# A fused attention and quantised linear layer: eight more score units among the projections, and a lead of 18 units in place of 14

## The chip, the cores and the metric

The kernel runs on one core of one Trainium2 chip. A core has engines with one instruction stream each, which meet through semaphores: PE (TensorE, matrix products into PSUM), DVE (VectorE), ACT (ScalarE), POOL (GpSimd) and SP (which here issues most DMAs). The metric is the device time of one execution in microseconds (us). The kernel before takes 1662.35 us, the median of three runs from 1661.26 to 1664.51 us. The profiled execution is another run of it.

## The reference, cut to what matters

The input `x` has 2 batches of 2048 tokens with 256 channels; there are 16 heads of 16 channels.

```python
q_in = linear(x, Wq);  Q = linear(concat[q_in, conv1d(q_in, 3 taps)], qproj)     # K in the same way
V = linear(x, Wv)
tau   = sigmoid(conv1d(gelu(depthwise_conv(x)), 1 tap))        # one number per token and head
delta = sigmoid(conv1d(gelu(depthwise_conv(x)), 1 tap))
scores = Q @ K.T / 4 * tau[query] + delta[key]
attn = softmax(scores) @ V
x = layernorm(x + linear(attn, out))
x = layernorm(x + fake_quant(x) @ fake_quant(weight).T + bias)
```

The softmax needs the maximum of each row of `scores`. The kernel computes every score twice: once with queries on the partitions, only to find the row maxima, and once with keys on the partitions, for the exponentials, with the maxima already subtracted inside the matrix product.

## The kernel before, in words

**Two blocks.** The first block (lines 355 to about 730) computes Q, K, V, tau and delta in 8 chunks of 512 tokens, here called chunk 0 to 7. All engines meet at its end. The second block is the loop: 32 iterations `i`, one for each group of four heads and 512 queries, four iterations to a group.

**A score unit** is a pair of matmuls (`s_unit`, the matmuls have line L227) that writes 128 queries by 512 keys for two heads at once into two PSUM banks, and one DVE `tensor_reduce` (`max_unit`, L237) that takes the maxima. An iteration's queries need 32 units, called (j, u) with u from 0 to 31 for iteration j. There are two pairs of banks, so unit s waits on PE until DVE has done the maximum of unit s-2 (semaphore `s_free`). The 1024 units and a few other pieces of work form one list, `items`, which PE and DVE go through in the same order.

**From maxima to rows.** For each j, POOL does 8 folds (`fold`, L248 and L251, four small instructions each), then `split_max` (L85 and L89 on `nm_pad`). DVE then transposes the result (`rows_turn`, L268) and SP stores it as extra rows beside the queries (`rows_store`, L279). DVE waits in `rows_turn(j-1)` for the semaphore `nm_ready`, and this call stands in DVE's program right behind the maximum of unit (j, 1), wherever that unit stands. POOL's folds for j = 0 stand in its program at the head of chunk 7, behind the last `q_sp` work of chunk 6 (L89 on `q_sp`); those for j = 1 stand at the start of the loop, behind a run of small bias copies (L1310 to L1320).

**Where units are done.** Some units are done early, in the first block. `PRE_STEP` says how many at each of 15 places of a chunk: places 0 to 2 and 3 to 5 are behind each six matmuls of the two K projections (L681), 6 behind the first half of the values (L695), 10 behind the second half, 7 to 9 and 11 to 13 in the two Q projections, 14 behind the pointwise product for the next chunk (L704). `DVE_PLACES` sets the points of DVE's order at which the maxima of these places stand, between its convolution taps (L525) and evacuations (`k_lows` L531, `v_bias` L539, `q_scale` L549). `PRE` is the sum, 42 units before.

**The loop's PE order.** An iteration has 32 slots. A slot has half the probabilities-times-values matmuls (`pv_half`, L918), two score matmuls for the exponentials (`st`, L905), and then as many items as `due` asks for: the items up to unit `LEAD` of iteration i+2, evenly over the slots. So iteration 0 does what is missing up to (2, LEAD), 36 units before; others do 32, and iteration 30 does the rest up to (31, 31) in 20 slots. ACT does the exponentials (L1048). `FOLD_AHEAD = LEAD // 4` tells POOL how many folds of the next j it does ahead.

Of the kernel before, what the change touches and what calls it, by code (L numbers as in the profile page):

```python
# [121 lines left out]
def layer_kernel(nc, t, out):  # L122
# [10 lines left out]
    with ExitStack() as top:  # L133
# [40 lines left out]


        UNITS = HH * TT * NQ
        LEAD = 14
        DEFER = 2
        W_AT, FT_AT = (22, 0), (25, UNITS // 2)
        O_AT = {(28 + n, 8 * a + 5): ("o", n, a) for n in range(3) for a in range(TT)}  # L180
# [1 line left out]
        for j in range(NIT):  # L182
            for u in range(UNITS):
# [3 lines left out]
                if (j, u) in O_AT:  # L187
                    items.append((j, O_AT[j, u]))
        FOLD_AHEAD = LEAD // 4
        FOLD_ORDER = [(qt, jh) for qt in range(TT) for jh in range(HH)]  # L190
# [139 lines left out]
        TD_BANK = 3  # L330
        COMBOS = [(k, c, r) for c in range(CT) for r in range(2) for k in range(2)]
        PAIR_AT = lambda *places: [2 * int(p in places) for p in range(15)]
        PRE_STEP = {2: PAIR_AT(10, 14)} | {n: PAIR_AT(6, 10, 14) for n in range(3, 7)} | {7: PAIR_AT(0, 2, 4, 6, 8, 10, 12)}
        DVE_PLACES = ((0, 1, 2), (3, 4, 5), (6,), (7, 8, 9), (10,), (11, 12, 13), (14,))
        pre_at, PRE = {}, 0
        for n, counts in PRE_STEP.items():
            for place, count in enumerate(counts):
# [460 lines left out]
        with ExitStack() as s3:  # L798
# [56 lines left out]
            with nc.Block() as block:  # L855
                @block.tensor
                def _(pe):
# [122 lines left out]
                    for i in range(NIT):  # L980
                        goal = items.index((i + 2, LEAD)) if i + 2 < NIT else len(items)
                        due = goal - issued
# [476 lines left out]
```

## Time and profile before

| | us |
|---|---|
| median of three runs | 1662.35 |
| profiled execution: device time | 1652.92 |
| its span | 1651.1 |
| PE busy | 1603.3 (97%) |
| DVE busy, of it the maxima L237 (1024 of them) | 1528.7 (93%), 1239.1 |
| ACT busy, of it the exponentials L1048 | 1311.1 (79%), 1109.0 |
| POOL busy | 448.0 (27%) |
| first block ends, loop's first matmul starts | 249.76 |
| last unit's maximum ends | 1515.8 |

The profile is one execution. Its engines are nearly all busy, and the share of busy time does not tell which of them sets the pace in a stage; the rows in time order do, by what each instruction waited for. "Releaser" in a row is the instruction that ended an idle time. Lines in the rows are those of the kernel.

### The profile page before, as it was taken

The numbers are of one execution on the slowest core, as the hardware profiler recorded it, in microseconds if no ns is written. First come the engines' busy times: TensorE is split into PE (matmuls) and PEld (weight loads), VectorE is DVE, ScalarE is ACT, GpSimd is POOL, SyncE is SP. The second block draws the span as 40 slices with busy tenths as digits, with TensorE's granted clock in tenths as the row PEclk, the third lists the DMA queues.
The fourth block names the chain that finished last, engine by engine and source line by source line (L and its number), as shares of the span: only waits on it lengthen the run. The fifth ranks groups of instructions, "written<-read, shape, count | busy, mean of one in ns | idle before, by whom it ended". The sixth has DMA issues, their size and how long they took to land.

```text
span 1651.1 us, 34599 instructions
## 1 busy us (share of the span) xinstructions
PE 1603.3 (97%) x13839; PEld 716.9 (43%) x13844; DVE 1528.7 (93%) x1616; ACT 1311.1 (79%) x2375; POOL 448.0 (27%) x1189
## 2 busy tenths in 40 slices
PE   8999999999999999999999999999999999999986
PEld 7767763333333333333333333333333343433465
DVE  5789887999999999999999999999999999988887
ACT  2876837888888888888888888888888877778645
POOL 4222246222222222222222222222232222331200
PEclk9999998999999999999999999999999999999999
DMA  3376427000700060015003400432152001000312
GB/s 114 108 182 157 142 82 113 8 8 9 87 8 8 19 76 8 15 25 70 8 9 37 60 8 9 49 48 56 37 63 32 8 8 43 25 27 20 115 60 90
DMA packets 55385, 84.79 MB, mean 51 GB/s; under 512 B 14524, under 2 KB 25404, under 8 KB 53852
## 3 DMA queue, kind: packets, MB, share of 16 engines
q1 hardware_dynamic: 53368, 82.49, 24.3%
q8 instruction: 108, 1.77, 0.5%
q14 instruction: 53, 0.43, 0.1%
q10 hardware_dynamic: 1856, 0.09, 0.1%
HBM read 51.36 MB, written 30.67 MB: 50 GB/s over the span
## 4 chain that ended last, share of the span: by engine, by line
PE 67%; DVE 14%; ACT 2%; issue 2%; ACTq 0%; DVEq 0%
PE ps L918 30%; PE ps L905 23%; PE ps L227 12%; DVE mx L237 10%; PE ps L864 1%; ACT e L1048 1%; ACT ev L1037 1%; DVE stats L1149 1%; PE ps L862 1%; DVE work L1208 0%; DVE work L1197 0%; DVE small L1192 0%; PE ps L861 0%; DVE work L1205 0%; DVE xq L1211 0%
## 5 line engine op out<-in xcount | busy, mean ns | idle before, releaser
L237 DVE TENSOR_REDUCE mx<-ps 128x2 f32<-128x1024 f32 x1024 | 1239.1, 1223 | 49.7 <-PE ps L227 36.9
L1048 ACT ACTIVATE e<-ps 128x512 f32<-128x512 f32 x2048 | 1109.0, 596 | 207.6 <-PE ps L905 167.0
L918 PE MATMUL ps<-e,v_grp 128*32 128x256 f32 x8192 | 655.8, 392 | 5.8 <-ACT ev L1037 5.8
L905 PE MATMUL ps<-q,k 52*128 52x512 f32 x2048 | 525.6, 500 | 4.5 <-PEq L355 4.3
L227 PE MATMUL ps<-k,q 50*128 50x512 f32 x2048 | 414.5, 399 | 4.5 <-DVE mx L237 3.9
L248 POOL TENSOR_SCALAR mn<-mx 128x1 f32<-128x1 f32 x512 | 180.5, 359 | 847.4 <-DVE mx L237 847.1
L905 PEld LDWEIGHTS ps<-q,k 52*128 52x128 f32 x2048 | 200.0, 184 | 430.7 <-ACT e L1048 388.0
L918 PEld LDWEIGHTS ps<-e,v_grp 128*32 128x32 f32 x8192 | 161.7, 108 | 377.7 <-issue 202.7
L227 PEld LDWEIGHTS ps<-k,q 50*128 50x128 f32 x2048 | 196.8, 187 | 18.4 <-DVE mx L237 10.3
L251 POOL TENSOR_SCALAR nm<-mn,mx 128x1 f32<-128x1 f32 x512 | 141.7, 289 | 25.2
L681 PE MATMUL ps<-x_p,m_p 128*128 128x512 f32 x576 | 142.6, 402 | 0.0
L681 PEld LDWEIGHTS ps<-x_p,m_p 128*128 128x128 f32 x576 | 107.2, 190 | 33.2 <-issue 8.1
L525 DVE SCALAR_TENSOR_TENSOR hid<-x_c,dw_w,hid 128x512 f32<-128x512 f32 x128 | 103.8, 862 | 14.1 <-ACT hid L466 14.1
L472 ACT ACTIVATE hid<-hid 128x512 f32<-128x512 f32 x64 | 40.4, 632 | 51.3 <-DVE hid L525 50.1
L1327 POOL TENSOR_TENSOR v_all<-v_all 128x1024 f32<-128x1024 f32 x8 | 20.4, 2562 | 100.7 <-DMA v_all<-rz_rows 100.7
L466 ACT ACTIVATE hid<-x_c,dw_b,dw_w 128x512 f32<-128x512 f32 x64 | 46.7, 804 | 0.2
L89 POOL TENSOR_TENSOR q_sp<-qx,q_sp 128x512 fp32r<-128x512 f32 x16 | 20.5, 1284 | 69.6 <-ACT q_sp L515 69.0
L89 POOL TENSOR_TENSOR x_p<-x_c,x_p 128x1028 fp32r<-128x1028 f32 x8 | 19.4, 2420 | 61.4 <-ACT x_p L460 61.3
L864 PE MATMUL ps<-wo_t,v_all 128*128 128x256 f32 x128 | 33.4, 384 | 0.0
L704 PE MATMUL ps<-hid,pw_w 128*16 128x512 f32 x128 | 30.2, 594 | 0.1
L971 PE MATMUL ps<-fw_p,xq_t 128*128 128x256 f32 x128 | 19.1, 306 | 8.9 <-ACT xq_t L1030 8.9
L864 PEld LDWEIGHTS ps<-wo_t,v_all 128*128 128x128 f32 x128 | 24.9, 194 | 3.6
(138 smaller groups left out, 611.6 us busy)
## 6 DMA issues: line engine op xcount, KB each, us to landing
k<-k_parts SPq DMA_DIRECT2D x42, 256.0 KB
q<-q_parts SPq DMA_DIRECT2D x84, 128.0 KB
k_parts<-k_sp SPq DMA_DIRECT2D x16, 512.0 KB, 4.9
q_parts<-q_sp SPq DMA_DIRECT2D x16, 512.0 KB, 4.1
att<-ev SPq DMA_DIRECT2D x32, 256.0 KB
x_c<-in_x_t SPq DMA_DIRECT2D x8, 514.0 KB, 5.8
tau_r<-tau_rows SPq DMA_DIRECT2D x16, 256.0 KB
q<-nm_rows SPq DMA_DIRECT2D x256, 2.0 KB
```

The source lines that it names most:

```text
L227: last = nc.tensor.matmul(ps[:, s_bank(s) + half, :], q_set[r, g % 2, j % NQ, jh, qt * P:(qt + 1) * P], k_set[r, g % 2, jh, kc * CH:(kc + ...
L237: nc.vector.tensor_reduce(mx[:, j % 2, :, jh, qt, kc], ps[:, b0:b0 + 2, :], AX.X, ALU.max).then_inc(s_free, 1)
L248: nc.gpsimd.tensor_scalar(mn[:, r:r + 1], parts[:, 0:1], parts[:, 1:2], parts[:, 2:3], ALU.max, ALU.max).then_inc(mx_folded, 1)
L251: nc.gpsimd.tensor_scalar(nm[:, r:r + 1], mn[:, r:r + 1], parts[:, 3:4], -1.0, ALU.max, ALU.mult).then_inc(nm_max, 1)
L466: nc.scalar.activation(hid[:, k, c, r], x_c[:, n % 2, c, 1:1 + CH], ACT.Identity, bias=dw_b[:, k, c, r:r + 1], scale=dw_w[:, k, c, r, 1:2] ...
L472: nc.scalar.activation(hid[:, k, c, r], hid[:, k, c, r], ACT.Gelu).then_inc(gelu_done, 1)
L525: nc.vector.scalar_tensor_tensor(y_, x_c[:, n % 2, c, which:which + CH], dw_w[:, k, c, r, which:which + 1], y_, ALU.mult, ALU.add).then_in ...
L681: mm = nc.tensor.matmul(ps[:, o, :], m_p[:, kw, side, c, tap, P * o:P * (o + 1)], x_p[:, n % 2, kx_, c, tap:tap + CH], start=(m == 0), sto ...
L864: last = nc.tensor.matmul(dst, a_t[p][:, c, P * a:P * (a + 1)], wo_t[:, c, :], start=False, stop=(c == CT - 1))
L905: nc.tensor.matmul(ps[:, st_bank(n), :], k_set[r, g % 2, jh, kt * P:(kt + 1) * P], q_set[r, g % 2, i % NQ, jh, :], start=True, stop=True). ...
L918: last = nc.tensor.matmul(ps[32 * h:32 * (h + 1), 0, PVW * part:PVW * (part + 1)], v_grp[:, kt, h, :], e[:, x % E_BUFS, h * CH + PVW * par ...
L1048: nc.scalar.activation(e[:, x % E_BUFS, h * CH:(h + 1) * CH], ps[:, st_bank(n), :], ACT.Exp).then_inc(e_ready, 1)
```

## The change

Two constants are changed. In the first block, place 3 of the chunks 4, 5 and 6 and place 14 of chunk 7 now have a pair of units each, so `PRE` is 50. `LEAD` is 18, so iteration 0 has 82 - 50 = 32 units in place of 36, iteration 30 has 14 in place of 18, and every other iteration has 32 as before. `FOLD_AHEAD` becomes 4. Because units are numbered in order, the pairs also carry other units than before: (1, 0) and (1, 1) are now done at place 14 of chunk 6.

```diff
         UNITS = HH * TT * NQ
-        LEAD = 14
+        LEAD = 18
         DEFER = 2
...
         PAIR_AT = lambda *places: [2 * int(p in places) for p in range(15)]
-        PRE_STEP = {2: PAIR_AT(10, 14)} | {n: PAIR_AT(6, 10, 14) for n in range(3, 7)} | {7: PAIR_AT(0, 2, 4, 6, 8, 10, 12)}
+        PRE_STEP = {2: PAIR_AT(10, 14), 3: PAIR_AT(6, 10, 14)} | {n: PAIR_AT(3, 6, 10, 14) for n in range(4, 7)} | {7: PAIR_AT(0, 2, 4, 6, 8, 10, 12, 14)}
```

DVE's order from the end of chunk 6 into chunk 7. `mx` are the maxima, `nm_rows<-nm_pad` is the transpose of `rows_turn(0)`, which waits for POOL's `nm_ready`, and `k_sp` is K's evacuation.

```order
 L549 SCALAR_TENSOR_TENSOR qx<-ps,side_bias,tau_r 128x512 [waits q_split,tau_loaded,q_full] x2
-L237 TENSOR_REDUCE mx<-ps 128x2 [waits s_full] x6
-L531 SCALAR_TENSOR_TENSOR k_sp<-ps,side_bias,k_sp 128x511 [waits k_high]
-L531 SCALAR_TENSOR_TENSOR k_sp<-ps,side_bias,k_sp 128x1
 L237 TENSOR_REDUCE mx<-ps 128x2 [waits s_full] x2
 L268 STREAM_TRANSPOSE nm_rows<-nm_pad 128x32 [waits nm_ready]
+L237 TENSOR_REDUCE mx<-ps 128x2 [waits s_full] x4
+L531 SCALAR_TENSOR_TENSOR k_sp<-ps,side_bias,k_sp 128x511 [waits k_high]
+L531 SCALAR_TENSOR_TENSOR k_sp<-ps,side_bias,k_sp 128x1
+L237 TENSOR_REDUCE mx<-ps 128x2 [waits s_full] x2
```

The transpose, and with it the wait for POOL, has moved ahead of six maxima and one evacuation; it now stands right behind the last pair of chunk 6. POOL's order in the first block is the same as before.

DVE's order over the end of the first block into the loop; `nm_max` is set by POOL's folds.

```order
 L549 SCALAR_TENSOR_TENSOR qx<-ps,side_bias,tau_r 128x511 [waits q_split,tau_loaded,q_full]
 L549 SCALAR_TENSOR_TENSOR qx<-ps,side_bias,tau_r 128x1
+L237 TENSOR_REDUCE mx<-ps 128x2 [waits s_full] x2
 L355 UNCONDITIONAL_BRANCH
 L1078 UNCONDITIONAL_BRANCH [waits barrier_Pool_Activation_PE_DVE_SP_release]
-L237 TENSOR_REDUCE mx<-ps 128x2 [waits s_full] x22
+L237 TENSOR_REDUCE mx<-ps 128x2 [waits s_full] x14
 L237 TENSOR_REDUCE mx<-ps 128x2 [waits s_full,nm_max]
 L237 TENSOR_REDUCE mx<-ps 128x2 [waits s_full]
```

The next instruction is the transpose of `rows_turn(1)`. It stood behind 24 maxima of the loop and now stands behind 16.

PE's order in chunk 5: the K projections, then the values.

```order
 L681 MATMUL ps<-x_p,m_p 128x512 x17
 L681 MATMUL ps<-x_p,m_p 128x512 [waits q_evac]
-L681 MATMUL ps<-x_p,m_p 128x512 x17
+L681 MATMUL ps<-x_p,m_p 128x512 x5
+L227 MATMUL ps<-k,q 128x512 [waits s_free]
+L227 MATMUL ps<-k,q 128x512
+L227 MATMUL ps<-k,q 128x512 [waits s_free]
+L227 MATMUL ps<-k,q 128x512
+L681 MATMUL ps<-x_p,m_p 128x512 x12
 L695 MATMUL ps<-wv_p,x_p 128x256 [waits v_evac]
```

One pair of units is new behind the first six matmuls of the second K projection; the pair of place 6 still follows behind the values.

## Rows read from the trace of the kernel before

**Rows 1.** The page's costliest group; busy us, mean ns, idle before and its releaser.

```profile
L237 DVE TENSOR_REDUCE mx<-ps 128x2 f32<-128x1024 f32 x1024 | 1239.1, 1223 | 49.7 <-PE ps L227 36.9
```

**Rows 2.** Stage table around chunk 5: us, busy of PE, PEld, DVE, ACT, POOL; PEclk, DMA, GB/s.

```profile
170.00:195.00 25.00, 25.00 (x123) 17.44 (x122) 22.75 (x28) 18.69 (x26) 6.60 (x4) 1.00 0.43 125
```

**Rows 3.** Timeline of PE in chunk 5: start, us, what [idle before].

```profile
167.70 8.68 PE L681 MATMUL ps<-x_p,m_p 128*128 128x512 f32 x36
...
177.72 0.73 PE L227 MATMUL ps<-k,q 50*128 50x512 f32 x4
178.38 4.47 PE L681 MATMUL ps<-x_p,m_p 128*128 128x512 f32 x18
...
189.25 3.61 PE L704 MATMUL ps<-hid,pw_w 128*16 128x512 f32 x16
```

**Rows 4.** Timeline of DVE in chunk 5.

```profile
174.18 2.87 DVE L525 SCALAR_TENSOR_TENSOR hid<-x_c,dw_w,hid 128x512 f32<-128x512 f32 x4
...
178.43 2.35 DVE L237 TENSOR_REDUCE mx<-ps 128x2 f32<-128x1024 f32 x2
180.69 4.30 DVE L525 SCALAR_TENSOR_TENSOR hid<-x_c,dw_w,hid 128x512 f32<-128x512 f32 x4
```

**Rows 5.** Timeline of POOL in chunk 5.

```profile
178.99 2.41 POOL L89 TENSOR_TENSOR x_p<-x_c,x_p 128x1028 fp32r<-128x1028 f32 x1 [9.91 <-ACT x_p L460]
```

**Rows 6.** Timeline of POOL, end of chunk 6 and the folds of j = 0.

```profile
217.66 2.65 POOL L89 TENSOR_TENSOR q_sp<-qx,q_sp 128x512 fp32r<-128x512 f32 x2 [8.86 <-ACT q_sp L515]
220.42 0.70 POOL L248 TENSOR_SCALAR mn<-mx 128x1 f32<-128x1 f32 x2
...
229.71 0.70 POOL L248 TENSOR_SCALAR mn<-mx 128x1 f32<-128x1 f32 x2
```

**Rows 7.** Timeline of DVE: last pair of chunk 6, and the transpose of j = 0.

```profile
219.08 4.62 DVE L237 TENSOR_REDUCE mx<-ps 128x2 f32<-128x1024 f32 x4 [1.57 <-PE ps L227]
...
231.66 0.21 DVE L268 STREAM_TRANSPOSE nm_rows<-nm_pad 128x32 f32<-128x32 f32 x1 [0.18 <-POOL nm_pad L89]
```

**Rows 8.** Timeline of PE in chunk 7: K projection and the pair of place 2.

```profile
221.93 3.07 PE L681 MATMUL ps<-x_p,m_p 128*128 128x512 f32 x12
224.93 0.73 PE L227 MATMUL ps<-k,q 50*128 50x512 f32 x4
```

**Rows 9.** Timeline of PE: the first row of the loop.

```profile
249.76 1.19 PE L905 MATMUL ps<-q,k 52*128 52x512 f32 x3 [4.27 <-PEq L355]
```

**Rows 10.** Stage table, PE alone: us, busy, PEclk, DMA, GB/s.

```profile
261.00:262.00 1.00, 1.00 (x12) 0.83 1.19 152
...
1602.00:1603.00 1.00, 1.00 (x8) 0.61 0.00 0
```

**Rows 11.** Timeline of PE near the end: work after an idle time.

```profile
1599.94 3.43 PE L971 MATMUL ps<-fw_p,xq_t 128*128 128x256 f32 x16 [7.03 <-ACT xq_t L1030]
```

**Rows 12.** Timeline of PE in iteration 0: slots 1, 2, 4, 5 and the units of slot 7.

```profile
256.05 1.08 PE L918 MATMUL ps<-e,v_grp 128*32 128x256 f32 x8
...
258.21 1.08 PE L918 MATMUL ps<-e,v_grp 128*32 128x256 f32 x8
...
262.05 0.64 PE L918 MATMUL ps<-e,v_grp 128*32 128x256 f32 x8
...
263.30 0.64 PE L918 MATMUL ps<-e,v_grp 128*32 128x256 f32 x8
...
266.68 0.98 PE L227 MATMUL ps<-k,q 50*128 50x512 f32 x4
```

**Rows 13.** Timeline of POOL: the first fold of j = 1, in the loop.

```profile
271.67 0.70 POOL L248 TENSOR_SCALAR mn<-mx 128x1 f32<-128x1 f32 x2 [0.23 <-POOL bias L1316]
```

**Rows 14.** Timeline of DVE: the transpose of j = 1, in iteration 0.

```profile
287.05 0.20 DVE L268 STREAM_TRANSPOSE nm_rows<-nm_pad 128x32 f32<-128x32 f32 x1
```

**Rows 15.** Timeline of PE in iteration 30: two slots without a unit.

```profile
1516.81 0.64 PE L918 MATMUL ps<-e,v_grp 128*32 128x256 f32 x8
...
1519.06 0.64 PE L918 MATMUL ps<-e,v_grp 128*32 128x256 f32 x8
```

## The prediction, made before the changed kernel was run

> **What bounds the kernel now.** I read the page's costliest groups first, then the stage tables and the timelines of PE, DVE and POOL in the first block and at the loop's start. The maxima are the costliest group, 1239.1 us [rows 1], and this invites the view that DVE sets the pace. It doesn't in general. In chunk 5 PE is busy for all 25.00 us and DVE for 22.75 [rows 2]: PE sets the pace, and DVE has about 2.2 us to spare. In the loop a slot with one unit takes 1.25 us from one L918 row to the next [rows 12], I use 1.24; DVE needs 2.35 us for two maxima that are ready, 1.13 apart, since one takes 1.22 and overlaps its neighbour by some 0.1 [rows 1, 4]. So there too DVE follows PE with some 0.1 us to spare. Only a slot with two units is different: two units back to back take 0.73 us from first start to last end and 0.66 to the next matmul, so 0.33 a unit, and one alone 0.40 [rows 3]; in such a slot the two take 0.98 [rows 12], as the second waits for a maximum. A second unit in a slot therefore costs 0.98 - 0.40 = 0.58.
>
> **The change, part by part.**
>
> *Three more pairs in the chunks 4 to 6 (place 3).* A pair costs PE 0.66 us, 177.72 to 178.38 [rows 3]. Three make 2.0. Their maxima stand behind the taps that end at 174.18 + 2.87 = 177.05 [rows 4], so both are done at 177.05 + 2.35 = 179.4. PE reaches the pair of place 6 at 177.72 + 0.66 = 178.38, and its second unit, 0.33 later at 178.71, needs the second of these maxima: PE waits 0.7 to 0.8. I take 0.8 for each of three chunks, 2.4 in all, between 0 (taps earlier) and 1.2. The maxima also push DVE 2.35 back, more than PE's 1.4 to 1.5 a chunk. What makes up for that: the next four taps took 4.30 us against 2.87 for four others, while POOL's L89 ran from 178.99 for 2.41 [rows 4, 5]. They now start at some 183, when that is over, so up to 1.4 us come back, DVE is about 1 us later than before, and its spare time covers it.
>
> The Trainium skill, "SBUF — State Buffer", "Who interferes with whom", states that a DVE instruction with two SBUF inputs and a GpSimd instruction that reads SBUF exclude each other, the second blocking until the first ends, while one that reads only PSUM isn't touched. By that the taps lose their 1.4 only where they meet POOL, and the relief is whole; without it DVE would be 2.4 late per chunk and the sum some 1 us a chunk higher. The trace's 4.30 against 2.87 agrees.
>
> So PE reaches chunk 7 2.0 + 2.4 = 4.4 us later, and so does the end of chunk 6 on POOL.
>
> *The wait for POOL at the end of chunk 6.* This is the term that decides. The transpose of j = 0 now stands behind the pair of place 14 of chunk 6. POOL has not begun the folds then: they start at 220.42, behind L89 on `q_sp` (217.66, 2.65 long), the eighth starts at 229.71, a fold each 1.33 us, and the transpose comes 1.95 after that, at 231.66, having waited for POOL 0.18 already [rows 6, 7]. All of it is later by 4.4, so the transpose is at 236.1. DVE's pair of chunk 6 is done at 219.08 + 2.35 + 4.4 = 225.8 [rows 7]: DVE idles some 10 us. Queued behind are the maxima of chunk 7's places 0 and 2 and K's evacuation. PE does the two units of place 0 without them, then its 12 matmuls, and stands at place 2 at 224.93 + 4.4 = 229.3 [rows 8], where the first unit needs a maximum that ends at 236.2 + 1.23 = 237.4. The second needs the next, 238.6, and ends at 238.9. Before, the pair was over at 224.93 + 0.66 = 225.6. PE's shift is 13.3, of which 4.4 were there: this wait costs 8.9. From there PE sets the pace again and nothing is given back, since in chunk 7 PE had no idle time behind place 2. I allow 7.5 to 10.
>
> *The clock.* PE idles 8 us there. At the loop's start PE had idled 4.27 us [rows 9], and ran at the lower level, 1.2 GHz, from 249.76 until 0.34 into the microsecond with 0.83 [rows 10], 11.6 us; near the end, after 7.03 idle, from 1599.94 until 0.78 into the microsecond with 0.61 [rows 10, 11], 2.8 us. At the lower level a slot takes 2.16 in place of 1.24 [rows 12], so 0.43 of the time is lost: 1.2 us or 5.0. The matmuls of chunk 7 are dense as in the short case, not broken up by exponentials as in the long one. I take 1.2; both ends are kept.
>
> The Trainium skill, "TensorE: Matmul & The Clock Gate", "HAM oscillation — how this bites in real kernels", puts the loss at the time at the lower clock times one half, and says that matmuls behind a long wait start cold each time. By it the term is 1.4, not 1.2, and it speaks against this change: the wait is paid twice. The granted clocks above agree that it happens.
>
> *The end of the first block.* The new pair at place 14 of chunk 7 is ready on PE before the last `q_scale` ends, but its maxima, 2.35, run behind it, beside ACT's and POOL's `q_sp` work, which is 1.3 a half on POOL alone [rows 6] and a little less on ACT. I take 0.2, between 0 and 2.35.
>
> *Iteration 0.* 36 units in 32 slots were four slots with two units. They go: 4 x 0.58 = 2.3 gained (a plain second unit would be 0.33, 1.3 in all).
>
> *A second wait for POOL, in iteration 0.* The transpose of j = 1 came behind 24 maxima, at 287.05 [rows 14], now behind 16. PE's times in the loop are told here as if it started as before. POOL starts these folds at 271.67, late because of its bias copies, and with one each 1.33 us the eighth starts at 281.0 and the transpose is possible 1.95 later, at 282.9 [rows 6, 13]. Before, the folds waited for the maxima and POOL's lateness was hidden. The 16th unit is in slot 15, its maximum over by 278.3: DVE idles 4.6 us. Two more units fit into the banks; that of slot 18 (266.68 + 11 x 1.24 = 280.3) needs the maximum that ends at 283.1 + 1.23 = 284.3. PE waits 4.0 us; the bound is 3 to 5. An idle time of 4.27 had lowered the clock, so I add 1.2 again, between 0 and 5.0.
>
> *Iteration 30.* Four slots lose their unit. Two without take 1519.06 - 1516.81 = 2.25 [rows 15], 1.125 each: 4 x (1.24 - 1.125) = 0.5 gained. All other iterations are the same, and the last unit is still issued in slot 20 of iteration 30, so the tail does not move by itself.
>
> **Sum.** 2.0 + 2.4 + 8.9 + 1.2 + 0.2 - 2.3 + 4.0 + 1.2 - 0.5 = +17.1 us. The profiled execution took 1652.92 us (span 1651.1), and would take 1670.0. The timed runs were 9.4 us above it, median 1662.35; I put the difference on the median: 1679.5 us.
>
> **The rivals.**
>
> *A, faster: DVE is the bound, and eight maxima leave the loop.* For it: L237 is the costliest group, and DVE is never long idle in the loop. Each would give 1.24, 9.9 in all, and cost PE 0.33 each in the first block, 2.6: 1655.0. It needs both transposes to find POOL done; against it stands the order of POOL, which has not begun the first fold when the first transpose is reached.
>
> *B, no wait matters.* If POOL's folds were hidden in both places but PE sets the pace: 4.4 + 0.2 - 2.3 - 0.5 = +1.8, 1664.2. The same objection.
>
> *C, only the first wait counts.* If POOL gets to the folds of j = 1 four microseconds earlier relative to PE, since its bias copies wait for DMAs that the first block's end may shift: 17.1 - 5.2 = +11.9, 1674.3.
>
> *D, the clock stays low as at the loop's start.* Both stretches last 11.6 us: + 2 x 3.8 = +24.7, 1687.1. For it: that is what iteration 0 showed once.
>
> **Chances.** The forecast 0.65, C 0.13, D 0.14, B 0.04, A 0.04. The forecast's own range, with the bounds above, is 1674 to 1686. The range that is to hold the time 8 times in 10 reaches to C and to D: 1672 to 1688. What can be told from no change is about 0.2%, 3.3 us. Faster by more than that has A alone, 0.04; within it B, with a small share of A, 0.04; slower 0.92.
>
> **What would show it.** In the profile of the changed kernel: an idle time of some 10 us of DVE ahead of the first L268, released by POOL `nm_pad`, and one of some 4.6 ahead of the second; on PE an idle time of some 8 us in chunk 7, released by an L237, and one of 4 in iteration 0; a granted clock below 1 behind each; the loop's first matmul at 249.76 + 4.4 + 8.9 + 1.2 + 0.2 = 264.5; slots of 1.24 in iteration 0 with none doubled. I am wrong if the first L268 follows its maximum without a wait, if the loop starts before 256, or if chunks 4 to 6 grow by more than 2 us each.

## The result and the profile after

The changed kernel took 1681.0 us (median of four runs, 1679.76 to 1685.26) against 1661.8 us for the kernel before (four runs beside it, 1651.45 to 1664.51). The ratio is 1.0134, interval 1.0105 to 1.0163. Repeated later with another set of runs it was 1.0148 (1.0105 to 1.0190). Executions that lay well above the others of the same kernel (up to 7261.69 us) are counted in the medians here and not in the ratios, which are not quotients of the medians (those would give 1.0116 for the first set). The forecast of 1679.5 us holds, and so does its mechanism for the most part, but that the sum came so near is partly luck: two terms were missing, and one that was forecast didn't appear in this form.

The profiled execution took 1680.37 us, span 1678.5. Against the profile of before that is 27.4 us, while the medians differ by 19.2: the execution of before that was profiled, 1652.92 us, lies low among its timed runs. "Before" and "after" below are these two profiles.

**The first wait.** Timeline of DVE from the last work of chunk 6 into chunk 7, after the change: start, us, what, [idle before, releaser].

```profile
223.23 2.36 DVE L237 TENSOR_REDUCE mx<-ps 128x2 f32<-128x1024 f32 x2 [1.63 <-PE ps L227]
235.74 0.21 DVE L268 STREAM_TRANSPOSE nm_rows<-nm_pad 128x32 f32<-128x32 f32 x1 [10.15 <-POOL nm_pad L89]
235.87 4.58 DVE L237 TENSOR_REDUCE mx<-ps 128x2 f32<-128x1024 f32 x4
240.36 0.87 DVE L531 SCALAR_TENSOR_TENSOR k_sp<-ps,side_bias,k_sp 128x511 fp32r<-128x511 f32 x2
```

The same stretch of POOL: the first fold starts behind the last `q_sp`, the eighth at 233.78.

```profile
221.75 2.64 POOL L89 TENSOR_TENSOR q_sp<-qx,q_sp 128x512 fp32r<-128x512 f32 x2 [9.52 <-ACT q_sp L515]
224.49 0.70 POOL L248 TENSOR_SCALAR mn<-mx 128x1 f32<-128x1 f32 x2
...
233.78 0.70 POOL L248 TENSOR_SCALAR mn<-mx 128x1 f32<-128x1 f32 x2
```

And of PE:

```profile
226.07 3.08 PE L681 MATMUL ps<-x_p,m_p 128*128 128x512 f32 x12
237.11 0.79 PE L227 MATMUL ps<-k,q 50*128 50x512 f32 x2 [7.96 <-DVE mx L237]
238.24 0.80 PE L227 MATMUL ps<-k,q 50*128 50x512 f32 x2 [0.34 <-DVE mx L237]
238.97 5.49 PE L681 MATMUL ps<-x_p,m_p 128*128 128x512 f32 x12
```

Read these three as one chain. POOL is where it was relative to its own inputs [rows 6], 4.1 us later in absolute time. DVE reaches the transpose ten microseconds before POOL has finished, where it used to arrive 0.18 us early [rows 7]. PE gets its two units of place 0 done and then stands before the pair of place 2 for 7.96 us [rows 8]. The next 12 matmuls take 5.49 us where the 12 ahead of the wait took 3.08: the clock has fallen. PE alone, stage table of after; us, busy, granted clock, DMA, GB/s:

```profile
244.00:245.00 1.00, 1.00 (x6) 0.63 0.00 0
...
285.00:286.00 1.00, 1.00 (x12) 0.65 1.10 217
...
1254.00:1255.00 1.00, 1.00 (x12) 0.50 1.10 131
```

The first of these rows is the end of the lower-clock stretch behind this wait (231 to 245). The second ends the one at the loop's start, which began at 265.2 and so held 20.5 us; in the profile of before it began at 247.7, while PE was idle, and held 13.7 us. The third belongs to a stretch that the kernel before doesn't have.

**The second wait**, in iteration 0, shrank to half a microsecond on DVE, and no PE row waits for it:

```profile
298.61 0.21 DVE L268 STREAM_TRANSPOSE nm_rows<-nm_pad 128x32 f32<-128x32 f32 x1 [0.54 <-POOL nm_pad L89]
```

**A stretch nobody had forecast**, iteration 24. Timeline of DVE in after:

```profile
1240.53 0.75 DVE L1094 TENSOR_SCALAR fw<-ps,act_factor 128x512 f32<-128x512 f32 x1 [0.36 <-PE ps L889]
1241.32 2.05 DVE L85 CAST fw_p<-fw 128x512 fp32r<-128x512 f32 x1
1243.41 2.71 DVE L89 TENSOR_TENSOR fw_p<-fw,fw_p 128x512 fp32r<-128x512 f32 x1
```

The same three instructions in before:

```profile
1227.49 0.75 DVE L1094 TENSOR_SCALAR fw<-ps,act_factor 128x512 f32<-128x512 f32 x1 [0.36 <-PE ps L889]
1228.28 0.43 DVE L85 CAST fw_p<-fw 128x512 fp32r<-128x512 f32 x1
1228.75 0.69 DVE L89 TENSOR_TENSOR fw_p<-fw,fw_p 128x512 fp32r<-128x512 f32 x1
```

POOL beside them, first after, then before:

```profile
1240.71 4.87 POOL L1327 TENSOR_TENSOR v_all<-v_all 128x1024 f32<-128x1024 f32 x2
```

```profile
1222.39 4.71 POOL L1327 TENSOR_TENSOR v_all<-v_all 128x1024 f32<-128x1024 f32 x2
```

and PE in after:

```profile
1247.31 0.80 PE L227 MATMUL ps<-k,q 50*128 50x512 f32 x2 [4.15 <-DVE mx L237]
```

Before, POOL's pair of L1327 was over at 1227.10, 1.2 us ahead of DVE's cast. Now the piece `ft` (the second linear layer's weight, prepared by L1094, L85 and L89) stands four units, about four slots, earlier relative to POOL's work, both lie on top of each other, and DVE's two instructions last 4.76 us in place of 1.12. PE waits 4.15 us for the next maximum, and its clock is at the lower level for 10.2 us (1244.9 to 1255.1). PE works again from 1247.31, so 7.8 us of that stretch are work; at 1 - 1.24 / 2.16 = 0.43 of the time [rows 12] they cost another 3.3. Together that is 7.5 of the 7.8 us by which the iteration is longer. The Trainium skill, "SBUF — State Buffer", "Who interferes with whom", says that a DVE cast in a 2-port mode, or a DVE instruction with two SBUF inputs, and a GpSimd instruction that reads SBUF shut each other out for a whole instruction. The trace agrees: POOL's two instructions end at 1243.09 and 1245.58, and the cast ends 0.28 us behind the first, the other DVE instruction 0.54 behind the second, each a little less than its own short duration.

**Where the 27.4 us between the two profiles lie**, by PE's rows in the first block and by the first L1037 (ACT's evacuation) of each iteration. The prediction's terms stand beside it.

| stretch | before | after | difference | predicted |
|---|---|---|---|---|
| ahead of chunk 4 | 141.95 | 142.26 | +0.3 | 0 |
| chunks 4 to 6 | 77.26 | 81.09 | +3.8 | +4.4 |
| chunk 7: wait, pair and slow matmuls | 10.03 | 21.86 | +11.8 | +10.1 |
| rest of the block | 20.52 | 20.52 | 0.0 | +0.2 |
| loop's start to L1037 of iteration 0 | 48.66 | 50.50 | +1.8 | +2.9 |
| iterations 1 to 23 | | | +0.5 | 0 |
| iteration 24 | 40.34 | 48.15 | +7.8 | 0 |
| iterations 25, 29 and 31 | | | -0.4 | 0 |
| iterations 26 to 28 | 137.59 | 141.45 | +3.9 | 0 |
| iteration 30 | 42.07 | 41.90 | -0.2 | -0.5 |
| behind iteration 31 | 71.0 | 68.9 | -2.0 | 0 |

**Iterations 26 to 28**, PE. In before the item `o` (L861 to L864, the output projection) shares its slot with a unit, which the row ahead of it shows:

```profile
1344.14 0.40 PE L227 MATMUL ps<-k,q 50*128 50x512 f32 x2
1344.63 0.28 PE L861 MATMUL ps<-bias,ones 128*128 128x256 bf16 x1
```

In after it has a slot to itself, and another slot therefore gets two units:

```profile
1366.13 0.28 PE L861 MATMUL ps<-bias,ones 128*128 128x256 bf16 x1
...
1371.02 0.99 PE L227 MATMUL ps<-k,q 50*128 50x512 f32 x4
```

The `o` items are tied to units (`O_AT`, u = 8a+5), and the slot in which an extra item falls is fixed by `LEAD`. With 14 both met; with 18 they don't.

### The profile page after: what moved, and what is told of

The parts are those of the page before. It is cut to its first block, busy times and chain, and to the rows that moved or that the text cites. A ratio compares the mean times of both kernels' runs of the same rounds, so it can differ in the third digit from the quotient of the medians.

```text
span 1678.5 us, 34599 instructions
## 1 busy us (share of the span) xinstructions
PE 1621.7 (97%) x13839; PEld 722.9 (43%) x13844; DVE 1529.0 (91%) x1616; ACT 1311.4 (78%) x2375; POOL 447.0 (27%) x1189
## 4 chain that ended last, share of the span: by engine, by line
PE 71%; DVE 10%; ACT 2%; issue 1%; ACTq 0%; DVEq 0%
PE ps L918 32%; PE ps L905 25%; PE ps L227 12%; DVE mx L237 5%; PE ps L864 1%; ACT e L1048 1%; ACT ev L1037 1%; DVE stats L1149 1%; PE ps L862 1%; DVE work L1208 0%; DVE small L1192 0%; PE ps L861 0%; DVE work L1197 0%; DVE work L1205 0%; DVE mv L1155 0%
## 5 line engine op out<-in xcount | busy, mean ns | idle before, releaser
L918 PE MATMUL ps<-e,v_grp 128*32 128x256 f32 x8192 | 661.6, 395 | 6.3 <-ACT ev L1037 6.1
L905 PE MATMUL ps<-q,k 52*128 52x512 f32 x2048 | 528.5, 503 | 3.4 <-PEq L355 3.1
L227 PE MATMUL ps<-k,q 50*128 50x512 f32 x2048 | 419.9, 405 | 19.1 <-DVE mx L237 18.3
L905 PEld LDWEIGHTS ps<-q,k 52*128 52x128 f32 x2048 | 200.7, 184 | 433.6 <-ACT e L1048 390.3
L918 PEld LDWEIGHTS ps<-e,v_grp 128*32 128x32 f32 x8192 | 162.4, 108 | 380.3 <-issue 211.8
L227 PEld LDWEIGHTS ps<-k,q 50*128 50x128 f32 x2048 | 198.5, 189 | 40.5 <-DVE mx L237 30.8
L681 PE MATMUL ps<-x_p,m_p 128*128 128x512 f32 x576 | 145.9, 408 | 0.0
L681 PEld LDWEIGHTS ps<-x_p,m_p 128*128 128x128 f32 x576 | 108.6, 193 | 34.3 <-issue 9.3
L1327 POOL TENSOR_TENSOR v_all<-v_all 128x1024 f32<-128x1024 f32 x8 | 20.4, 2559 | 100.5 <-DMA v_all<-rz_rows 100.5
L89 POOL TENSOR_TENSOR q_sp<-qx,q_sp 128x512 fp32r<-128x512 f32 x16 | 20.5, 1282 | 71.6 <-ACT q_sp L515 71.0
L89 POOL TENSOR_TENSOR x_p<-x_c,x_p 128x1028 fp32r<-128x1028 f32 x8 | 19.4, 2421 | 64.3 <-ACT x_p L460 64.2
L864 PE MATMUL ps<-wo_t,v_all 128*128 128x256 f32 x128 | 32.8, 379 | 0.0
L479 ACT ACTIVATE k_sp<-ps,side_bias 128x511 fp32r<-128x511 f32 (+2 forms) x24 | 12.1, 542 | 24.8 <-PE ps L681 24.5
L704 PE MATMUL ps<-hid,pw_w 128*16 128x512 f32 x128 | 30.2, 594 | 0.1
```

The costliest lines, as they stand in the source:

```text
L227: last = nc.tensor.matmul(ps[:, s_bank(s) + half, :], q_set[r, g % 2, j % NQ, jh, qt * P:(qt + 1) * P], k_set[r, g % 2, jh, kc * CH:(kc + ...
L681: mm = nc.tensor.matmul(ps[:, o, :], m_p[:, kw, side, c, tap, P * o:P * (o + 1)], x_p[:, n % 2, kx_, c, tap:tap + CH], start=(m == 0), sto ...
L864: last = nc.tensor.matmul(dst, a_t[p][:, c, P * a:P * (a + 1)], wo_t[:, c, :], start=False, stop=(c == CT - 1))
L905: nc.tensor.matmul(ps[:, st_bank(n), :], k_set[r, g % 2, jh, kt * P:(kt + 1) * P], q_set[r, g % 2, i % NQ, jh, :], start=True, stop=True). ...
L918: last = nc.tensor.matmul(ps[32 * h:32 * (h + 1), 0, PVW * part:PVW * (part + 1)], v_grp[:, kt, h, :], e[:, x % E_BUFS, h * CH + PVW * par ...
```

## The experiments

The theory: the time comes from where the first transpose stands, from the collision in iteration 24, and from the `o` items. The rivals: the clock at the loop's start by itself, or the new pairs by themselves. The kernel before ran beside each kernel, and the ratios are against these runs.

**The kernel before once more**, unchanged.

> The kernel before, unchanged, for a second profile of it. Its timed runs lie near 1662 us and its profiled one at 1652.9, while the changed kernel's profile agrees with its timed runs (1680). Theory P (a near miss): in iteration 24 POOL's two normalise instructions end at 1227.09 and DVE's cast of the ft item begins at 1227.49, 0.4 us later; where it is early by that much the two collide as they do in the changed kernel (cast 2.05 us in place of 0.43), and the run is some 8 to 10 us longer. Then a profile of a 1662 run shows the longer casts. Theory Q: the difference is in the granted clock at the start of the loop (11.6 us at the lower level in the one profile); then a profile of a 1662 run shows about 20 us there, and the casts are short. If the profile is again near 1652, neither is told apart by it.

Measured: 1657.74 us, ratio 0.9995 (0.9967 to 1.0024). Its profiled execution (span 1714.3 us, granted clock 0.844) is no example of either theory, though the cast L85 on `fw_p` was short there too, 0.42 us. The mean granted clock, which is on record for every execution, speaks for Theory Q. Of 22 executions of the kernel before, taken beside the last experiments, the fastest took 1650.13 us at 0.990 and the slowest 1667.30 us at 0.980. By an estimate from these figures the slower one spent 2 x (0.990 - 0.980) x 1660 = 33 us more at the lower clock (which is half the full one, hence the 2), which at 0.43 is 14 of the 17 us between them.

**The first transpose later.**

```diff
-                        if u == DEFER - 1 and j > 0:
+                        if (j, u) == (1, 7):
                             rows_turn(dve, j - 1)
```

> The changed kernel, but rows_turn(0) stands behind unit (1, 7) in place of (1, 1), so at place 4 of chunk 7, where it stood before the change. Everything else of the change stays. My theory (the wait for POOL's folds at the end of chunk 6 costs 8.9 us and the clock behind it 2.6): DVE's wait of 10.15 us ahead of the first L268 is gone, PE's of 7.96 in chunk 7 too, and the loop's first matmul comes at 254 to 254.5 in place of 265.7: 11.5 us less, 1669.5 us. The second wait for POOL, in iteration 0, may come back, since it was hidden by 20 us at the lower clock there: if the lower clock lasts 11.6 us again, PE waits up to 4 us and the time is 1670 to 1673. Rival (DVE is the bound, the pairs themselves cost): the work of the pairs is the same, so the loop starts at 262 or later and the time stays within 3 us of 1681.

Measured: 1676.2 us, 1.0109 (1.0078 to 1.0140). The first wait is gone, since the transpose of j = 0 now stands some six units later; timeline of DVE:

```profile
235.47 0.21 DVE L268 STREAM_TRANSPOSE nm_rows<-nm_pad 128x32 f32<-128x32 f32 x1 [0.20 <-POOL nm_pad L89]
...
286.33 0.21 DVE L268 STREAM_TRANSPOSE nm_rows<-nm_pad 128x32 f32<-128x32 f32 x1 [4.29 <-POOL nm_pad L89]
```

and PE starts the loop 12.2 us earlier than in after:

```profile
253.54 0.69 PE L905 MATMUL ps<-q,k 52*128 52x512 f32 x3 [3.13 <-PEq L355]
...
287.70 0.50 PE L227 MATMUL ps<-k,q 50*128 50x512 f32 x2 [3.46 <-DVE mx L237]
```

But the second rows of both fences show the other wait, which the changed kernel itself had all but lost: 4.29 us on DVE and 3.46 on PE, and behind it the clock stays at the lower level for 17.1 us, 289 to 306. From loop's start to L1037 of iteration 0 it takes 57.66 us, 7.2 more than in after. So of the 12.2 us some 7 were given back, and the time is above the 1670 to 1673 us that had been expected. This is the prediction's second wait, near the size predicted for it (4.6 and 4.0), and the lower clock behind it lasts longer than in the prediction's long case (11.6 us).

**The piece `ft` four units later**, out of POOL's way.

```diff
-        W_AT, FT_AT = (22, 0), (25, UNITS // 2)
+        W_AT, FT_AT = (22, 0), (25, UNITS // 2 + 4)
```

> The changed kernel, but the ft item (the transposed weight, whose result DVE scales and casts) stands behind unit (25, 20) in place of (25, 16). With a lead of 18 this puts it at the slot of iteration 24 at which a lead of 14 had it. Theory: in the changed kernel it meets POOL's two normalise instructions (cast 2.05 us for 0.43, the next 2.71 for 0.69), PE waits 4.15 us for DVE and then runs at the lower clock for some 10 us: 7.8 us in all in the profile. Then this run shows short casts, no PE wait in iteration 24, and 1673 us. Rival: the long casts come from DMA traffic of the group load in that window, not from POOL; then they stay long wherever they stand within it, and the time stays near 1681.

Measured: 1675.63 us, 1.0102 (1.0041 to 1.0163). DVE's cast is short again:

```profile
1247.14 0.46 DVE L85 CAST fw_p<-fw 128x512 fp32r<-128x512 f32 x1
1247.64 0.69 DVE L89 TENSOR_TENSOR fw_p<-fw,fw_p 128x512 fp32r<-128x512 f32 x1
```

and iteration 24 takes 40.33 us, as before the change (40.34), in place of 48.15. The waits of the first block are as in after (loop's start at 265.56). The collision is shown in the profile; the ratio's wide interval alone wouldn't have told it. The rival, DMA traffic, is out: in 1247.10 to 1248.30 of this profile the DMA engines are busy throughout (share 1.07) and the cast is short.

**Both edits together.**

> Both edits of the two kernels ahead of this one: rows_turn(0) behind (1, 7), ft behind (25, 20). If the two costs are independent, the gains add: 1681 - 11.5 - 7.8 = 1661.7 us, up to 1665 if the second wait for POOL comes back in iteration 0. This would be level with the kernel before (1661.8). Rival (DVE is the bound and eight maxima left the loop): 1655 or less.

Measured: 1667.82 us, 1.0048 (1.0024 to 1.0073), some 3 to 6 us above what had been expected. The loop starts at 257.14, 3.6 us later than with the first of the edits alone. This delay is there already in chunk 0 (the first L681 behind L704 at 51.43 against 47.84), and ahead of it, from 33.6 to 40.5, the clock was low in this profile and not in the other. Iteration 24 takes 40.33. L268 waits for POOL for 0.3 us in the whole execution: the clock was low for 23.9 us at the loop's start, the slow slots delayed the maxima, and the second wait hid behind them, as in after. The missing gain lies in iterations 26 to 28 (141.35 us against 137.59), which neither edit touches, and in more time at the lower clock.

**Both, and the second transpose eight units later**, on the reasoning that no wait for POOL would then be left.

```diff
-                            if u == DEFER - 1:
+                            if u == (DEFER + 7 if j == 2 else DEFER - 1):
```

> e3_both, and rows_turn(1) stands behind unit (2, 9) in place of (2, 1), so again behind 24 maxima of the loop as before the change. Both waits for POOL and the collision of the ft item are then out; what is left of the change are its pairs and its lead. My theory: left are +3.8 us in chunks 4 to 6 (three pairs on PE, and their maxima ahead of place 6), -2.3 for the doubled slots of iteration 0, -0.5 in iteration 30: +1 us against before, ratio 1.000 to 1.003, and the profile shows no idle DVE ahead of any early L268 whatever the length of the lower clock at the loop's start. Rival 1 (DVE is the bound): ratio 0.996 or less. Rival 2 (something else of the change costs as much as e3's distance of 8 us to before): ratio 1.004 to 1.006, as e3.

Measured: 1672.81 us, 1.0062 (1.0032 to 1.0091): no better than without the edit, and I had expected it to be. One cause is in PE's waits: the transposed rows now reach the score matmuls of iteration 1 too late,

```profile
297.87 0.50 PE L905 MATMUL ps<-q,k 52*128 52x512 f32 x2 [2.23 <-DMA q<-nm_rows]
```

and the clock fell again for 3.4 us behind this. So a transpose that comes too early waits for POOL, one that comes too late is waited for, and the room between is narrow. Two more causes are in iterations 26 to 28, 141.33 us against 137.59, which none of these edits touches, and in iterations 29 and 31, together about 5 us longer than in before, with the clock low for 17.1 us there against 3.4. The profiled execution took 1664.45 us, though. Three of the ten took 1658.29 to 1664.45 us at a granted clock of 0.986 to 0.991, the other seven 1671.79 to 1678.26 us at 0.979 to 0.984. What the seven had more goes with the lower clock; where it fell in them, no profile of this kernel shows.

**`LEAD` alone**: the 42 early units of before, `LEAD` 18, `ft` as above.

> The kernel before with LEAD = 18 alone (42 units among the projections as before, so iteration 0 does 40 units), and ft behind (25, 20), which keeps its slot. Theory: in iteration 0 eight slots are doubled in place of four, 4 x 0.58 = +2.3 us, iteration 30 gives 0.5 back: ratio 1.000 to 1.002; the first transpose is where it was, at 231.7. Rival (the lead of 18 by itself costs, through the order of folds and items in the loop): ratio 1.004 or more, with waits in the iterations 1 to 29 that the kernel before does not have.

Measured: 1663.35 us, 1.0024 (0.9998 to 1.0050). Its profiled execution had the clock low for 85 us at the loop's start (a row of it stands at the end of this document), so only its later part is used: iterations 26 to 28 take 141.45 us. That belongs to `LEAD`, not to the pairs.

**The kernel before with PE kept at work over the block's end**: 18 matmuls of 512 columns into a free bank, so that PE doesn't idle [rows 9].

```diff
+                pe.wait_ge(td_ready, NCHUNK)
+                for m in range(18):
+                    nc.tensor.matmul(ps[:, TD_BANK, :], m_p[:, 0, 0, 0, 0, 0:P], x_p[:, 1, 0, 0, 0:CH], start=True, stop=True)
```

> The kernel before, with 18 matmuls of 512 columns added on PE at the end of the first block, into a PSUM bank that nobody reads any more (their product is not used). They fill the 4.27 us in which PE waits for the other engines at the block's end. Theory: the lower clock at the loop's start (13.6 us in the profile before, 10 to 24 us in the others) comes from this idle time. Without it the loop starts at the same 249.8 and at the full clock; a slot takes 1.24 in place of 2.16 from the start and 5 to 6 us go: ratio 0.996 to 0.997, and the spread of the timed runs becomes smaller. Rival: the loop's first matmuls wait for ACT and are too thin, so the clock falls anyway; then the ratio is 1.000, or the matmuls themselves delay the block's end.

Measured: 1655.68 us, 0.9987 (0.9968 to 1.0007). Timeline of PE (its lines are three higher than those of before):

```profile
250.39 4.37 PE L741 MATMUL ps<-x_p,m_p 128*128 128x512 f32 x18
255.05 0.70 PE L908 MATMUL ps<-q,k 52*128 52x512 f32 x3 [0.29 <-PEq L355]
...
258.59 0.64 PE L921 MATMUL ps<-e,v_grp 128*32 128x256 f32 x8
...
259.82 1.08 PE L921 MATMUL ps<-e,v_grp 128*32 128x256 f32 x8
```

The idle time is 0.29 us, and slot 0 runs at full clock, 0.64 for eight L921. One slot later the same eight take 1.08: the clock fell all the same, and stayed low for 13.7 us, as long as in before. So the idle time at the block's end is not needed for the lower clock at the loop's start. What remains is the work there, L908 and L921 (the L905 and L918 of before) with short waits for ACT (0.45 us ahead of the second row of L908); that this is the reason is only argued.

But this profile is of the slowest of the ten executions (1665.87 us, granted clock 0.983). The other nine took 1654.21 to 1660.70 us at 0.986 to 0.992, and the ten together have a mean granted clock of 0.989, against 0.986 in the 31 executions of the kernel before beside them. The median is 4.8 us lower, close to the 5 to 6 us of the theory, and the interval of the ratio just reaches 1. Whether the filled gap shortens the lower-clock stretch in most executions stays open.

**The same 18 matmuls on the kernel of the fourth edit.**

> e4_no_waits with the same 18 matmuls at the end of the first block. Theory: as e6 against before: 5 us less than e4, ratio 0.996 to 0.998. It also tells whether the change, freed of its waits, beats the kernel before where both start the loop at the full clock: by my theory it is 1 us behind e6; by the rival that DVE is the bound it is 5 us or more ahead of e6.

Measured: 1670.81 us, 1.0065 (1.0040 to 1.0089), no different from 1.0062 without them, so here the filled gap gained nothing that shows. The lower clock came twice in the profile, 20.5 and 23.9 us. The second stretch began at 309.8, right behind the same wait for the rows of j = 1 as in the fourth edit, and reached into iteration 1 (48.11 us in place of 40.27):

```profile
308.74 0.50 PE L908 MATMUL ps<-q,k 52*128 52x512 f32 x2 [2.24 <-DMA q<-nm_rows]
```

With the transpose so late this wait is paid in both kernels, with 3.4 us of lower clock behind it in one profile and 23.9 in the other.

**The `o` items moved with `LEAD`**, the first transpose as above, the second only four units later, `ft` as above.

```diff
-        O_AT = {(28 + n, 8 * a + 5): ("o", n, a) for n in range(3) for a in range(TT)}
+        O_AT = {(28 + n + (a + 1) // TT, (8 * a + 9) % UNITS): ("o", n, a) for n in range(3) for a in range(TT)}
...
-                            if u == DEFER - 1:
+                            if u == (DEFER + 3 if j == 2 else DEFER - 1):
```

> The changed kernel with everything that hangs on the position of a unit moved along with the lead: rows_turn(0) behind (1, 7), rows_turn(1) behind (2, 5), ft behind (25, 20), and the twelve o items (the blocks of the output projection in iterations 26 to 29) four units later, so that they fall in the same slots as before. Found in the profiles of all runs with a lead of 18: iterations 26, 27, 28 take 43.1, 49.3, 48.9 us in place of 42.1, 47.8, 47.7, 3.8 us in all, because an o item no longer shares its slot with a unit and the doubled slot falls on two units. Theory: with this the iterations 26 to 28 are back at 42.1, 47.8, 47.7, no DVE waits for POOL ahead of an early L268 and PE does not wait for the rows of j = 1 (2.2 us in e4_no_waits). Left are +3.8 us in chunks 4 to 6, -2.3 in iteration 0, -0.5 in iteration 30: ratio 0.999 to 1.003. Rival: the ratio stays at 1.005 to 1.006 as in e3 and e4, so a cost remains that the shape of the slots does not explain, such as a longer lower clock at the loop's start after the changed end of the first block.

Measured: 1662.69 us, 1.0014 (0.9988 to 1.0040). No transpose waits longer than 0.28 us, iteration 0 keeps its order, and iterations 26 to 28 take 139.15 us, of which 3.4 us at the lower clock in iteration 28. With the 1.5 us that this costs (3.4 times 0.43, an estimate) taken off, 137.7, as before. The loss of the change is gone within what the measurement can tell, and no gain is left. Two things differ from the fourth edit, the `o` items and the place of the second transpose; the ratio alone doesn't part them, the iteration times do for the `o` items.

**The pairs alone**: 50 early units, `LEAD` 14, the first transpose later.

> The changed kernel with LEAD = 14, so only the eight more units among the projections, with rows_turn(0) behind (1, 7); iteration 0 does 28 units and no other iteration changes; ft and the o items are in their slots of before. rows_turn(1) stands behind 16 maxima, where POOL has not folded j = 1 yet: with 28 units over 32 slots the 16th is in slot 18, at some 281 if the loop starts as before, and POOL is ready at 282.9 (relative to a start at 249.8), so PE waits little. Theory: +3.8 in chunks 4 to 6; iteration 0 has 28 plain slots and 4 empty ones, -2.3 -0.5: ratio 1.000 to 1.003. Rival 1 (DVE is the bound and eight maxima fewer in the loop pay off): 0.996 or less. Rival 2: as in e8, a remaining cost at the loop's start, 1.005.

Measured: 1658.7 us, 0.9998 (0.9975 to 1.0021). Iterations 24 and 26 to 28 take 40.55 and 137.48 us. Eight more units among the projections cost nothing that can be measured, once the transpose isn't pulled ahead with them. Its loop starts at 257.40, but 3.8 us of that were there already in chunk 0, behind a lower-clock stretch as in the profile of both edits. Iteration 0 has 28 units then, and reaches its L1037 in 48.22 us although the clock was low for 17.1 us, 3.4 more than in before.

**The changed kernel once more.**

> The changed kernel, unchanged, for a second profile and for the times on this chip beside the others. Theory: ratio 1.011 to 1.016; DVE's wait of 10 us in chunk 7 and the long casts of iteration 24 (2.05 us) are there again, since both follow from the order; the second wait for POOL, in iteration 0, is 0 to 4.6 us long and is the longer the sooner the clock rises after the loop's start: about 0.5 with 20 us at the lower level, 4 or more with 10. Rival: the collision of iteration 24 is chance; then the casts are short this time.

Measured: 1684.36 us (1679.36 to 1687.29), 1.0148 (1.0105 to 1.0190). Timeline of DVE:

```profile
235.75 0.21 DVE L268 STREAM_TRANSPOSE nm_rows<-nm_pad 128x32 f32<-128x32 f32 x1 [10.23 <-POOL nm_pad L89]
...
299.27 0.21 DVE L268 STREAM_TRANSPOSE nm_rows<-nm_pad 128x32 f32<-128x32 f32 x1 [1.22 <-POOL nm_pad L89]
```

The waits repeat, and so does the cast, 2.06 us: the collision is in the order, not an accident of one execution. Iteration 24 took 46.27; the clock was low for only 3.4 us there. The four executions of the changed kernel have a mean granted clock of 0.979, those of the kernel before beside them 0.986. By the same estimate as above that is 23 us more at the lower clock, or 10 of the 25 us between the two kernels: a good part of what the change costs is clock and not idle time.

The stretches of all profiles side by side, us:

| kernel | loop's start | to L1037 of iteration 0 | iteration 24 | iterations 26 to 28 |
|---|---|---|---|---|
| before | 249.76 | 48.66 | 40.34 | 137.59 |
| changed | 265.73 | 50.50 | 48.15 | 141.45 |
| changed, again | 265.69 | 51.14 | 46.27 | 141.26 |
| first transpose later | 253.54 | 57.66 | 49.20 | 141.27 |
| `ft` later | 265.56 | 51.42 | 40.33 | 141.32 |
| both | 257.14 | 51.48 | 40.33 | 141.35 |
| both, second transpose 8 later | 253.08 | 50.30 | 40.33 | 141.33 |
| `o` items aligned, second transpose 4 later | 253.69 | 51.01 | 40.27 | 139.15 |
| pairs alone | 257.40 | 48.22 | 40.55 | 137.48 |

## Why the prediction was right, and where it was not

*What bounds it.* Right. PE sets the pace, and eight maxima fewer in the loop gave no 9.9 us; rival A and rival B are excluded by the wait of 10.15 us on DVE alone.

*The pairs in the chunks 4 to 6.* 3.8 us against 4.4. The sign that was asked for, less than 2 us each, holds. PE's wait in the pair of place 6, forecast at 0.8 a chunk, was 0.76, 0.16 and 0.40 us, 1.3 and not 2.4 in all; on the other hand the 36 matmuls of the K projections, now parted by the new pair, took 0.18 us more in each chunk, which the sum did not have. DVE's taps behind the new pair got faster, but less than foreseen: in chunk 5 four took 3.82 us where they had taken 4.30 [rows 4], 0.5 back and not 1.4.

```profile
181.97 2.35 DVE L237 TENSOR_REDUCE mx<-ps 128x2 f32<-128x1024 f32 x2
184.23 3.82 DVE L525 SCALAR_TENSOR_TENSOR hid<-x_c,dw_w,hid 128x512 f32<-128x512 f32 x4
```

```profile
181.74 2.41 POOL L89 TENSOR_TENSOR x_p<-x_c,x_p 128x1028 fp32r<-128x1028 f32 x1 [11.18 <-ACT x_p L460]
184.23 1.29 POOL L89 TENSOR_TENSOR d_sp<-td,d_sp 16x512 fp32r<-16x512 f32 x1
```

The prediction had left POOL where it was. It moved along by 2.75 us [rows 5], and the taps, free of its first L89, met the next one.

*The wait for POOL at the end of chunk 6.* Right in place, releaser and size: DVE 10.15 idle ("some 10"), PE 7.96 ("some 8"), this wait's cost 9.2 against 8.9, and the loop's first matmul at 265.73 against 264.5. The experiment with the transpose later took the loop's start from 265.73 to 253.54, 12.2 us, against 11.8 in the table.

*The clock behind it.* A term mis-sized. I took 1.2, the short case; it was 2.6 (6.24 us from 238.97 to 245.21, against 3.65 before). The matmuls there are as dense as in the case I took it from, but the lower level held longer.

*Iteration 0, the doubled slots.* Predicted -2.3. Three of the four doubled slots lie ahead of the L1037 at which the table ends the iteration, 3 x 0.58 = 1.7. But the lower clock held for seven slots at 2.16 where it had held for three, four times 0.9, which put 3.6 on top; together the +1.8 of the table.

*The second wait for POOL.* Predicted 4.0 + 1.2, with PE's times "as if it started as before". In after it was 0.5 us on DVE and nothing on PE, since the slow slots held the maxima back while POOL went on at its own speed. The experiment in which the loop starts at 253.54 has it with 4.29 us on DVE and 3.46 on PE, and 17.1 us of lower clock behind it where I had taken the short case. (The reason given there, that an idle time of 4.27 us "had lowered the clock", isn't borne out: with that gap filled the clock fell too.) So the mechanism is real and sits next to a lower-clock stretch that hides it: the two don't add. On this point rival C came out (only the first wait counts, 1674.3 us), by the clock and not by POOL's bias copies, which it had named.

*Iteration 30* gave 0.2 and not 0.5.

*What the prediction did not have.* I wrote "All other iterations are the same". This is the step that failed. A lead counted in units moves everything that is tied to a unit against everything that is tied to a slot or to another engine: `ft` onto POOL's L1327 (+7.8 in one profile, +5.9 in the other), and the `o` items out of their doubled slots (+3.9, of which iteration 29 returns about 1.2 where the clock is full: 46.35 in the changed kernel's second profile, 47.58 with `LEAD` 14 and the pairs). Both could be read from the order and from the times of before, ahead of any run. The 2.0 us gained behind iteration 31 have no cause that I could show. They don't come from the lead: this stretch takes 68.9 us with the pairs alone and 71.1 with the `o` items aligned.

*Why the total still fit.* Sum of the forecast +17.1. Add the missed terms (7.8 + 3.9), and take away what the second wait didn't cost (5.2), and the profile should show +23.6; the rest to 27.4 is mostly the clock, 1.4 in chunk 7 and 3.6 in iteration 0, less the 2.0 behind iteration 31. So the sum of 17.1 was short by 10 between the two profiles. The medians differ by 19.2 in the first set and by 24.9 in the last (1684.36 against 1659.46), so the true size lies nearer to 1.4% than to the forecast's 1.03%. That 1679.5 stands so close to the first median of 1681.0 is luck. The executions of one kernel spread by some 8 us either way, and most of it goes with the mean granted clock, as the kernel before shows above; in all profiles but one (85 us) the lower-clock stretch at the loop's start holds 10 to 24 us. What decides this length stays open.

## What to carry to other kernels

Before pulling work ahead in a fixed order, list what waits at points counted in that work: a blocking call that is keyed to a unit number moves with it, past the engine that should have answered. Then do the same for side jobs that share a port or a slot, far from the edit: here they cost 11.7 us, as much as the wait did with its clock. And a wait of PE is to be priced with the clock behind it: by estimate 1.5 us (3.4 x 0.43) here in the mildest case and 10.3 (23.9 x 0.43) in the worst, both behind a wait of 2.2 us for the same rows. One profile doesn't give this price; the granted clocks of all executions should be read beside it.

## What the runs showed of the hardware

- The granted clock fell without a long idle time ahead of it. With PE filled over the block's end there were gaps of 0.29 and 0.45 us; it went to 1.2 GHz one slot into the loop and stayed there 13.7 us with PE busy. In the profile of the kernel with `LEAD` alone it was low in stage rows like this one, PE busy in the whole of it:

```profile
320.00:330.00 10.00, 10.00 (x58) 0.50 0.07 27
```

- The Trainium skill, "TensorE: Matmul & The Clock Gate", "What's actually happening", sets the level by how busy PE has been lately. The trace agrees behind the wait in chunk 7: there the full clock was back 7.6 us after PE had resumed at 237.11. It doesn't at the loop's start: there, with matmuls of 52 rows (L905), 50 rows (L227) and 32 columns (L918) where most matmuls of chunk 7 have 128 of each, and PE busy for 19.7 of the 20.0 us, it took these 20 us. The measurement decides; whether the small shapes are the reason was not tried.
- A DVE cast of 128x512 took 2.05 us beside POOL's L1327 and 0.43 alone; a two-input DVE instruction of the same size 2.71 and 0.69.
